# Three dense taps with x in four blocks of sixteen, gathered groups multiplied in pairs, rings of three: a deformable convolution behind a selective scan

## The reference

```python
offset = conv3x3(g, offset_w); mask = sigmoid(conv3x3(g, mask_w))   # g = group norm of x
# for each of 9 taps k and each pixel: position (y, x) = pixel + tap + offset
val = bilinear(g, y, x) * mask            # four corners, zero outside the image
out = einsum('op,bphw->bohw', weight, val)  # 9 taps x 32 channels -> 32 channels
x = x + out
```

## Time and profile before

| | |
|---|---|
| median of 3 runs | 1050.22 us (1049.63 to 1051.04) |
| the profiled execution's own time | 1048.38 us |
| its span | 1046.6 us |
| mean granted clock of PE | 0.806 of full speed |
| busy, share of the span | PE 77%, DVE 73%, POOL 58%, ACT 28% |

### The profile page before, as it was taken

How to read it: one execution, slowest core, us unless ns; L and a number is a source line. 1 busy time by engine, 2 the same in 40 slices (tenths; PEclk the granted TensorE clock), 3 DMA queues, 4 the chain that set the end, 5 groups by cost and what they waited for, 6 DMA issues and landing times.

```text
span 1046.6 us, 8464 instructions
## 1 busy us (share of the span) xinstructions
PE 808.5 (77%) x2556; PEld 405.3 (39%) x2557; DVE 767.5 (73%) x1047; ACT 295.6 (28%) x408; POOL 603.7 (58%) x560
## 2 busy tenths in 40 slices
PE   3346858587878687578888878592799999999997
PEld 1123323132322135354444444242655545454444
DVE  4889742899999587789999999859764545546463
ACT  1020155845443155112111211000312313131310
POOL 0000000177763077877777777777777777777774
PEclk9657978799999696668687777765588998798886
DMA  4000017000000721121111111273535343444432
GB/s 118 0 0 1 0 30 164 2 0 1 0 1 0 153 65 46 40 54 50 50 52 51 50 52 52 62 196 88 136 93 151 93 132 92 107 117 116 109 91 53
DMA packets 31699, 69.83 MB, mean 67 GB/s; under 512 B 12240, under 2 KB 12496, under 8 KB 30544
## 3 DMA queue, kind: packets, MB, share of 16 engines
q1 hardware_dynamic: 14416, 33.17, 12.4%
q0 software_dynamic: 16384, 33.59, 12.3%
q10 hardware_dynamic: 864, 2.64, 1.1%
HBM read 54.94 MB, written 5.77 MB: 58 GB/s over the span
## 4 chain that ended last, share of the span: by engine, by line
POOL 45%; issue 16%; DVE 12%; PE 6%; DMA 4%; ACT 1%; POOLq 0%; ACTq 0%; DVEq 0%
POOL got L773 45%; DVE scratch L1125 6%; DVE scratch L1132 3%; DMA got<-corner_table,idx_slot 2%; DVE prodg L784 1%; PE PS L1008 1%; PE PS L865 1%; PE PS L866 1%; DMA G<-XN 1%; PE PS L1225 1%; PE PS L874 1%; PE PS L1001 1%; PE PS L993 1%; PE PS L884 0%; DMA got<-corner_table,idx_all 0%
## 5 line engine op out<-in xcount | busy, mean ns | idle before, releaser
L773 POOL DMA_INDIRECT got<-corner_table,idx_slot x432 | 424.9, 984 | 131.7 <-issue 128.6
L1425 PE MATMUL PS<-scratch 128*128 128x512 f32 (+1 forms) x320 | 174.6, 693 | 8.1 <-DVE scratch L1407 8.0
L808 PE MATMUL PS<-ln_g,w 128*128 128x32 f32 x1024 | 164.1, 322 | 0.0
L808 PEld LDWEIGHTS PS<-ln_g,w 128*128 128x128 f32 x1024 | 158.8, 244 | 0.0
L993 PE MATMUL PS<-parts,selb 96*128 96x512 bf16 (+1 forms) x256 | 89.6, 451 | 83.2 <-DVE scratch L1051 43.3
L1008 PE MATMUL PS<-scratch,wt 128*128 128x512 f32 x256 | 146.6, 703 | 0.5 <-DVE scratch L1132 0.5
L773 POOL DMA_INDIRECT got<-corner_table,idx_all x80 | 86.3, 1079 | 62.1 <-DVE prime L1299 38.0
L1425 PEld LDWEIGHTS PS<-scratch 128*128 128x128 f32 (+1 forms) x320 | 64.7, 219 | 106.0 <-issue 96.5
L781 DVE COPY idx_slot<-idx_all 128x9 uint32<-128x9 uint32 (+1 forms) x64 | 12.4, 193 | 119.8 <-DMA got<-corner_table,idx_slot 96.0
L1506 POOL MEMSET w<- 128x1152 f32 x1 | 1.1, 1057 | 159.2 <-POOLq L596 159.2
L993 PEld LDWEIGHTS PS<-parts,selb 96*128 96x128 bf16 x256 | 23.1, 117 | 157.4 <-DVE scratch L1051 56.4
(11 more groups left out here) (334 smaller groups left out, 1157.9 us busy)
## 6 DMA issues: line engine op xcount, KB each, us to landing
UZ<-dense_rows SPq DMA_DIRECT2D x16, 512.0 KB, 3.6
UZ<-dense_rows SPq DMA_DIRECT2D x64, 128.0 KB, 4.5
got<-corner_table,idx_slot POOLq DMA_INDIRECT x432, 2.5
XN<-ln_g SPq DMA_DIRECT2D x6, 256.0 KB, 5.6
got<-corner_table,idx_all POOLq DMA_INDIRECT x80, 2.5
corner_table<-scratch SPq DMA_DIRECT2D x1, 1056.0 KB, 10.3
corner_table<-XN SPq DMA_DIRECT2D x1, 1056.0 KB, 10.7
X<-in_x SPq DMA_DIRECT2D x4, 256.0 KB, 4.9
```

What stands on the lines that cost most here:

```text
L773: pool.indirect_dma_start(got[:, slot, tap, :, :].rearrange("p k c -> p (k c)"), None, tables[b], bass.IndirectOffsetOnAxis(ap=index[:, ta ...
L808: last = nc.tensor.matmul(group_psum(slot), w3[:, t, :], colgs[slot][:, t * C:t * C + C], start=False, stop=(t == n - 1))
L1425: last = nc.tensor.matmul(PS[:, 2 * k + h, :], steps[rows, j, 4 * h:4 * h + 4, :].rearrange("p b c -> p (b c)"), ramps[k][rows, j, :], sta ...
```

## The change

Three taps instead of two are dense, so image 1's groups gather six taps instead of seven. The x range is cut into four blocks of sixteen columns instead of eight of eight; the slopes of a block fill nine products instead of five, and the four blocks with 32 channels fill 128 output rows, so a batch is nine products in one accumulation instead of two halves of five, with one pick and one sum. There are 24 batches instead of 16, three for every four turns. The masks of a batch are four rows, each broadcast to 32 partitions, instead of eight. Loads, ramps and hats have three buffers instead of two (`RING`); the pick and the sum of a batch follow two batches behind its products instead of one (`LAG`); ACT prepares two batches ahead. The groups of image 1 are transposed into a buffer for two groups, and PE multiplies two groups at once with 64 columns. `dense_first` waits for the steps before the first load.

```diff
-DENSE = 2
+DENSE = 3
-SLOPES = 5
+SLOPES = 9
+RING = 3
+LAG = 2
...
-        load = [sem(f"dense_load{k}") for k in range(2)]
+        load = [sem(f"dense_load{k}") for k in range(RING)]
...
+        def pair_weigh(v, G):
+            n, m, slot = NEAR, (G - GROUPS) // 2, G % SLOTS
+            v.wait_ge(gathered[slot], landed(G))
...
+            v.wait_ge(l3["o_psum"], 2 * m + 35)
+            nc.vector.transpose(pairs[m % 2][:, :, G % 2, :], colsum[:, 0:n * C].rearrange("p (t c) -> p t c", c=C)).then_inc(l3["col_done"], 1)
+
+        def pair_multiply(pe, m):
+            pe.wait_ge(l3["col_done"], GROUPS + 2 * m + 2)
+            pe.wait_ge(l3["o_read"], max(33, 2 * m + 32))
+            nc.tensor.matmul(pair_psum(m), ident, pair_pixels(m), start=True, stop=False)
+            for t in range(NEAR):
+                last = nc.tensor.matmul(pair_psum(m), w3[:, t, :], pairs[m % 2][:, t, :, :].rearrange("p s c -> p (s c)"),
+                                        start=False, stop=(t == NEAR - 1))
+            last.then_inc(l3["o_psum"], 2)
...
         def dense_first(sp):
...
-            sp.wait_ge(de["steps_out"], 1)
+            sp.wait_ge(de["table_done"], 1)
...
             sp.wait_ge(de["rows_in"], 16)
+            sp.wait_ge(de["steps_in"], 16)
 
         def dense_load(sp, n):
             half, q, d = BATCHES[n]
-            k, cols = n % 2, slice(half * BANK, (half + 1) * BANK)
-            if n >= 2:
-                sp.wait_ge(de["ramps"], 6 * (n - 1))
-                sp.wait_ge(de["t_used"], 2 * (n - 1))
-            sp.dma_start(loads[k][:, 0:2, :], rows_dram[q, 10 * d:10 * d + 2, cols].partition_broadcast(P)).then_inc(load[k], 16)
+            k, cols = n % RING, slice(half * BANK, (half + 1) * BANK)
+            if n >= RING:
+                sp.wait_ge(de["ramps"], (SLOPES + 1) * (n - RING + 1))
+                sp.wait_ge(de["t_used"], n - RING + 1)
+            sp.dma_start(loads[k][:, 0:2, :], rows_dram[q, 6 * d:6 * d + 2, cols].partition_broadcast(P)).then_inc(load[k], 16)
             for i in range(4):
-                sp.dma_start(loads[k][32 * i:32 * i + 32, 2:4, :],
-                             rows_dram[q, 10 * d + 2 + i:10 * d + 10:4, cols].partition_broadcast(32)).then_inc(load[k], 16)
+                sp.dma_start(loads[k][32 * i:32 * i + 32, 2, :], rows_dram[q, 6 * d + 2 + i, cols].partition_broadcast(32)).then_inc(load[k], 16)
...
         def dense_pick(v, n):
-            k = n % 2
-            v.wait_ge(load[k], 80 * (n // 2 + 1))
-            if n:
-                v.wait_ge(de["sum_psum"], n)
-            for h in range(2):
-                v.wait_ge(de["t_psum"], 2 * n + h + 1)
-                nc.vector.tensor_tensor(picked[:, h, :], PS[:, 2 * k + h, :], loads[k][:, 2 + h, :], ALU.mult).then_inc(de["t_used"], 1)
+            k = n % RING
+            v.wait_ge(load[k], 80 * (n // RING + 1))
+            if n >= 2:
+                v.wait_ge(de["sum_psum"], n - 1)
+            v.wait_ge(de["t_psum"], n + 1)
+            nc.vector.tensor_tensor(picked[n % 2], PS[:, n % 4, :], loads[k][:, 2, :], ALU.mult).then_inc(de["t_used"], 1)
...
             @block.tensor
...
+                    elif G % 2 == 0:
+                        m = (G - GROUPS) // 2 - 1
...
+                        pair_multiply(pe, m)
                     for n in batches_after(G):
                         dense_sample(pe, n)
-                        if n:
-                            dense_sum(pe, n - 1)
+                        if n >= LAG:
+                            dense_sum(pe, n - LAG)
...
             @block.scalar
...
-                        if n == 0:
-                            dense_scalar(act, 0)
-                        if n + 1 < len(BATCHES):
-                            dense_scalar(act, n + 1)
+                        for k in range(0 if n == 0 else n + 2, min(n + 3, len(BATCHES))):
+                            dense_scalar(act, k)
...
             @block.vector
...
                         dense_weights(v, n)
-                        if n:
-                            dense_pick(v, n - 1)
+                        if n >= LAG:
+                            dense_pick(v, n - LAG)
```

More of the change, by code:

```diff
@@ L730, in build @@
         colgs = [g[:, k * COL:(k + 1) * COL] for k in range(SLOTS)]
-        colsum = g[:, SLOTS * COL:(SLOTS + 1) * COL]
+        colsum = g[:, SLOTS * COL + 96:(SLOTS + 1) * COL + 96]
         w3 = sb("w3", [P, TAPS, P])
@@ L738, in build @@
                                              "prods", "t_psum", "t_used", "sum_psum", "added")}
-        load = [sem(f"dense_load{k}") for k in range(2)]
+        load = [sem(f"dense_load{k}") for k in range(RING)]
         rows_dram = nc.dram_tensor("dense_rows", (4, C, QUARTER), F32, kind="Internal").ap()
[L742 to L750, removed]
+        xn_flat = XN[:, :, :].rearrange("p b n -> p (b n)")
+        ramps = [t.rearrange("p (j n) -> p j n", j=SLOPES)
+                 for t in (xn_flat[:, 0:SLOPES * BANK], scratch[:, 0:SLOPES * BANK], scratch[:, SLOPES * BANK:2 * SLOPES * BANK])]
+        hats = [xn_flat[:, 4608 + BANK * k:4608 + BANK * (k + 1)] for k in range(RING)]
+        picked = [xn_flat[:, 6144 + BANK * k:6144 + BANK * (k + 1)] for k in range(2)]
+        loads = [UZ[:, 1024 + 1536 * k:1024 + 1536 * (k + 1)].rearrange("p (r n) -> p r n", r=3) for k in range(RING)]
+        steps_odd = UZ[:, 1024:2048].rearrange("p (j b c) -> p j b c", j=8, c=C)
+        fields_t = UZ[:, 5632:6656]
+        fields = UZ[:, 6656:7680].rearrange("p (g k) -> p g k", k=C)
+        steps = UZ[:, 6656:6656 + SLOPES * 4 * C].rearrange("p (j b c) -> p j b c", j=SLOPES, c=C)
+        w3_rows = UZ[:, 7840:7840 + DENSE * C].rearrange("p (d o) -> p d o", o=C)
         BATCHES = [(half, q, d) for half in (1, 0) for q in range(4) for d in range(DENSE)]
@@ L816, in tensor_turn, with pair_out @@
+        def pair_out(act, m):
+            act.wait_ge(l3["o_psum"], GROUPS + 2 * m + 2 + SLOTS)
+            nc.scalar.activation(pair_pixels(m), pair_psum(m), ACT.Copy).then_inc(l3["o_read"], 2)
         def tensor_turn(pe, G):
@@ L835, in vector_turn @@
         def vector_turn(v, G):
-            if G < B * GROUPS:
+            if G >= GROUPS:
+                pair_weigh(v, G)
+            else:
                 group_weigh(v, G, G % SLOTS, landed(G), near(G))
@@ L1346, in dense_fields @@
             vchain(v, nc.vector.tensor_copy(row(0), y))
-            vchain(v, nc.vector.scalar_tensor_tensor(row(1), blk, -8.0, x, ALU.mult, ALU.add))
-            for k in range(8):
+            vchain(v, nc.vector.scalar_tensor_tensor(row(1), blk, -16.0, x, ALU.mult, ALU.add))
+            for k in range(4):
                 vchain(v, nc.vector.scalar_tensor_tensor(row(2 + k), blk, float(k), msk, ALU.is_equal, ALU.mult))
@@ L1352, in dense_table @@
         def dense_table(v):
[L1354 to L1362, removed]
+            at = tabs[1][64:P, :, 0, :].rearrange("p (b j s) c -> p s j b c", b=4, s=2)
+            up = slice(64, P)
+            nc.vector.tensor_tensor(steps_odd[up, :, :, :], at[:, 1], at[:, 0], ALU.subtract).then_inc(de["steps_out"], 1)
+            v.wait_ge(de["rows_out"], 1)
+            nc.vector.tensor_copy(steps[up, 0, :, :], at[:, 0, 0])
+            nc.vector.tensor_tensor(steps[up, 1:8, :, :], at[:, 0, 1:8], at[:, 1, 0:7], ALU.subtract)
+            nc.vector.tensor_tensor(steps[up, 8, 0:3, :], at[:, 0, 0, 1:4], at[:, 1, 7, 0:3], ALU.subtract)
+            nc.vector.tensor_scalar(steps[up, 8, 3, :], at[:, 1, 7, 3], -1.0, None, ALU.mult)
             nc.vector.tensor_reduce(w3_rows, w3[:, NEAR:TAPS, :].rearrange("p t (q o) -> p t o q", q=4), AX.X, ALU.add
@@ L1417, in dense_sample @@
                 pe.wait_ge(l3["below_ready"], 4 * B)
-            else:
-                pe.wait_ge(de["t_used"], max(2 * (n - 1), 1))
-            for h in range(2):
[L1421 to L1427, removed]
@@ L1429, in dense_pick @@
-        def dense_pick(v, n):
-            k = n % 2
-            v.wait_ge(load[k], 80 * (n // 2 + 1))
-            if n:
-                v.wait_ge(de["sum_psum"], n)
-            for h in range(2):
-                v.wait_ge(de["t_psum"], 2 * n + h + 1)
-                nc.vector.tensor_tensor(picked[:, h, :], PS[:, 2 * k + h, :], loads[k][:, 2 + h, :], ALU.mult).then_inc(de["t_used"], 1)
+            if n >= 4:
+                pe.wait_ge(de["t_used"], n - 3)
+            for j in range(SLOPES):
+                rows = up if j == SLOPES - 1 else slice(0, P)
+                pe.wait_ge(de["prods"], SLOPES * n + j + 1)
+                last = nc.tensor.matmul(PS[:, n % 4, :], steps[rows, j, :, :].rearrange("p b c -> p (b c)"),
+                                        ramps[k][rows, j, :], start=(j == 0), stop=(j == SLOPES - 1))
@@ L1439, in dense_sum @@
+            last.then_inc(de["t_psum"], 1)
+        def dense_pick(v, n):
+            k = n % RING
[4 more added lines that the diff above has]
```

(33 more changed lines are left out.)

49 lines of the change are left out of this document (35 added, 14 removed).

## The result

The changed kernel takes 1083.56 us (median of four runs, 1081.63 to 1085.33) against 1049.93 before. The ratio on record is 1.0311, with a 95% interval of 1.0281 to 1.0341 (the two medians as they stand divide to 1.0320). It is slower, by 3.1% where 5.3% was forecast. The profiled execution's span is 1083.1 us.

A forecast was written before the change was run, and what follows sets the result against it. It took the closed loop of load, ACT, products and pick as the bound: 0.07 + 6.0 + 1.88 + 6.0 + 0.68 = 14.63 us, 21 times; with start, stores and tail span 1102.1, median 1106 us, 5.3% slower; range 1070 to 1136.

The forecast's parts named there:

- The loop stays closed since ring and lag grow together: Dense batches: load n still starts behind the products of n-1; load, ACT, products, pick take 14.63 us per batch.
- The load, 6.0 us: Dense batch, load issue to ACT's start: 7.0 us before, less 0.97 for 256 KB saved; bounds 4.3 and 7.0.
- the forecast's floor of 4.3: Lower bound of the load: last transfer issued some 1.8 us after the first, plus 2.5 us to land.
- Nine products, 6.0: DVE's products of a dense batch, paced by ACT's ramps: 9 x 0.668 = 6.0 us.
- The 0.668 of the forecast: DVE's time per product behind ACT's ramps, from 3.34 / 5 in the kernel before; 0.636 where ramps lie ready.
- From ACT's start to the first product, 1.88: Dense batch: the first product follows ACT's start after 1.88 us, as before.
- the pick, 0.68: End of a dense batch on DVE: the pick is one instruction, 0.65 plus 0.03 us.
- Start, stores, tail: Outside the loops: first pick at 772.7, some 2 us once for image 0's stores, pick 21 at 1081.9, span end 1102.1.
- Hidden work: Beside the loop: 32 removed gathers give nothing, DVE's group work fits the gap, PE needs 10.6 of 14.6 us.
- rival B: PE at low clock sets the pace: mild form 8 us more, 1114; hard form 1238; chance of over 1136, 0.05.
- Rival A at 1025: Loads hidden, loop open: POOL (1009) or PE decides, median 1025; needs a loop under 10.4 to 10.6 us; chance 0.07.

The follow-up runs named there:

- experiment 1: The changed kernel with the pick and sum one batch behind the products (LAG 1 instead of 2), three buffers kept: 1012.94 us, ratio 0.965 to the kernel before.
- experiment 7: The changed kernel with y and x rows of a load not waiting for the pick, only the masks: 1011.72 us, ratio 0.9646 to the kernel before.
- experiment 6: The changed kernel with two buffers, a lag of one and ACT one batch ahead: 1084.24 us, ratio 1.0332 to the kernel before.
- experiment 2: The changed kernel with two dense taps instead of three (seven gathered taps, 16 batches): 1051.82 us, ratio 1.0006 to the kernel before.
- experiment 4: The changed kernel with loads from batch 3 on leaving out their four mask transfers: 1050.25 us, ratio 0.9989 to the kernel before.
- experiment 3: The changed kernel with image 1's groups multiplied one by one, without pairs: 1098.31 us, ratio 1.0449 to the kernel before.

## Why the prediction was right, and where it was off

- *The loop stays closed since ring and lag grow together*: shown. Experiments 1 and 7 open it at two places and fall to 1013 and 1012; experiment 6 takes one from each and stays at 1084; experiment 2 shows that it needs the third tap to matter.
- *The load, 6.0 us*: the term of the sum that was mis-sized. It is 5.15. The forecast priced the 256 KB saved at the mean rate of the whole load, 0.97, and measured are 1.85. SP issues five transfers in either kernel, in 1.8 to 1.9 us from the first to the start of the last, so the saving lies behind the issues. A part is less gathering beside a load: where POOL gathers without a pause, as before, in experiments 1 and 2, the new load takes 5.57 and 5.55. That leaves some 1.4 for the smaller masks and 0.4 for the gathers, a split that is worked out from means and not tested by itself. In all -0.85 x 21 = -18. (The row under the forecast's floor of 4.3 is of four transfers issued together, not of a lone one; the floor wasn't reached.)
- *Nine products, 6.0*: 5.76 on the mean with the step to the pick (5.75 from 813.45 to 819.20). The 0.668 of the forecast was a mean over five products, start included; it doesn't hold for nine, which take 5.72 / 9 = 0.636 each. -0.24 x 21 = -5.
- *From ACT's start to the first product, 1.88, and the pick, 0.68*: 1.89 and 0.70.
- *Start, stores, tail*: pick 0 ends at 774.9 instead of 772.7, since DVE worked on the products of three batches and on two groups without a gap (751.5 to 774.2); the load behind the stores took 8.15 us to ACT's start, 3 over the others (2 were forecast); the tail is 19.1 instead of 20.2. Together: 774.9 + 289.1 + 19.1 = 1083.1, against 772.7 + 309.2 + 20.2 = 1102.1.
- *Hidden work*: POOL's idle time is put down to DVE, as said. PE had its idle time, and the clock fell in it: on PE's timeline of the changed kernel, the samples that take longer all follow a pause, though not every pause does it.

```profile
814.28 8.16 PE L1469 MATMUL PS<-scratch,UZ 128*128 128x512 f32 x18 [0.69 <-DVE scratch L1454]
...
841.52 9.85 PE L1469 MATMUL PS<-scratch,UZ 128*128 128x512 f32 x18 [2.83 <-DVE scratch L1454]
...
1045.11 8.16 PE L1469 MATMUL PS<-scratch,UZ 128*128 128x512 f32 x18 [1.97 <-DVE scratch L1454]
...
1058.39 11.12 PE L1469 MATMUL PS<-scratch,UZ 128*128 128x512 f32 x18 [2.45 <-DVE scratch L1454]
```

  The mean granted clock is 0.91 of the full 2.4 GHz from 770 to 990 us, where the open loop has 0.99 to 1.00. The Trainium skill's account that rival B names ("TensorE: Matmul & The Clock Gate", section on HAM oscillation) is of a kernel in which every burst behind a wait began at the slow clock; the trace agrees in part, since here some bursts do (9.85 to 11.17 us) and some don't (8.16). Up to pick 21 the slow samples lie in PE's slack, and no pick waits for PE. The last ones, 11.12 us, don't: behind them DVE waits 1.3 for PE at the last pick and 2.8 at the last addition, and the tail is 2.4 longer than in experiment 4, whose last samples took 8.16. Rival B had the mechanism, and the bound only in the tail.
- *Rival A at 1025*: the case that experiments 1 and 7 made was cheaper, 1012 to 1013. Samples took 8.16 instead of 8.5, and the span's tail behind the last sample was shorter than the 14.3 taken (996.1 to 1009.6 with LAG 1). The pace that it gave POOL and PE, 10.4 and 10.6 per batch, came out at 10.2 to 10.3 per load. Experiment 4's loop of 12.2, still over it, stayed closed, as A says.

## What to carry to other kernels

In these runs a deeper ring helped only by the amount by which it exceeds the lag of the reader that frees it: in lists that run in order, write down behind which instruction the freeing one stands. When the bound is to be cut, price the latency loops that fitted beside it: before, this one had 4 us to spare and stood on no chain. A wait on one engine's list also holds what stands behind it for others, as ACT's write-outs held PE in experiment 3.

## What the runs showed of the hardware

A product with 64 columns cost no more than one with 32: 12 records at full clock took 1.50 us in the pairs of the changed kernel, and 1.50 for single groups in experiment 3, so two groups in a pair cost what one costs alone. That fits a price set by the weight loads, which are busy for 23.3 of the 24.7 us that PE spends on these records of pairs; it wasn't tested by itself.

```profile
812.09 1.50 PE L852 MATMUL PS<-ln_g,w 128*128 128x64 f32 x12
```

```profile
817.49 1.50 PE L812 MATMUL PS<-ln_g,w 128*128 128x32 f32 x12
```
